# New issue orders for seven of eight attention groups, and the mixture's weights computed in the fourth group

## The reference

```python
xn = layernorm(x)
Q, K, V = heads(xn @ Wqkv); Q, K = rope(Q), rope(K)
attn = softmax(where(causal, Q @ K.T * scale, -inf))
a = (attn @ V) @ Wout + bout
probs = softmax(xn @ gate_w.T + gate_b)
weights, selected = top_k(probs, 2)
true_weights = weights * (selected < 8)
norm_w = true_weights / where(sum(true_weights) > 0, sum(true_weights), 1)
m = sum over the two selected of norm_w * (xn @ expert_w[e] + expert_b[e])
out = x + a + m
```

## Time and profile before

| what | value |
|---|---|
| median of 3 runs | 1015.39 us (1014.62 to 1016.34) |
| the profiled execution | 1015.35 us, its span 1013.6 us |
| PE, DVE, ACT, POOL busy | 90%, 83%, 72%, 46% of the span |
| groups 1 and 2 (plain, route) | 91.1 and 93.1 us |
| groups 3 to 6 (experts) | 105.8, 106.4, 106.7, 105.9 us |
| group 7 (plain) | 96.0 us |
| group 8 (last), to the last normalisation | 91.5 us |

### The profile page before, as it was taken

One profiled execution on the slowest core, in us unless ns is written; L12 is line 12 of the kernel. 1 busy time (PEld: TensorE's weight loads), 2 busy tenths in 40 slices (PEclk: granted clock), 3 DMA queues, 4 the chain that ended last, 5 costly groups with the idle time before them and its releaser, 6 DMA issues. The chain is left out here.

```text
span 1013.6 us, 22104 instructions
## 1 busy us (share of the span) xinstructions
PE 909.3 (90%) x7874; PEld 389.5 (38%) x7874; DVE 846.4 (83%) x1096; ACT 727.5 (72%) x1542; POOL 462.7 (46%) x588
## 2 busy tenths in 40 slices
PE   3888445999999999999999999999999799999988
PEld 1544311333433244344443544353434233323257
DVE  6999789899889988886888788877888599994856
ACT  3556200888778888888888788878887688799922
POOL 4677659555200343344834564255222344355610
PEclk9999765899999999999999999999999899999989
DMA  9776810300200323244413542265323321022113
GB/s 324 267 256 238 285 51 6 111 2 26 68 14 2 106 85 126 78 135 145 126 54 114 151 143 76 70 167 134 82 75 118 97 60 54 23 64 64 43 42 125
DMA packets 82084, 106.65 MB, mean 105 GB/s; under 512 B 10000, under 2 KB 59064, under 8 KB 80952
## 3 DMA queue, kind: packets, MB, share of 16 engines
q1 hardware_dynamic: 74488, 85.83, 26.3%
q0 software_dynamic: 6528, 17.83, 6.7%
q10 hardware_dynamic: 960, 1.57, 0.5%
HBM read 67.37 MB, written 37.50 MB: 103 GB/s over the span
## 5 line engine op out<-in xcount | busy, mean ns | idle before, releaser
L1272 DVE TENSOR_REDUCE blk<-psP 128x2 f32<-128x1024 f32 (+2 forms) x576 | 640.9, 1161 | 102.1 <-PE psP L1415 52.0
L1218 ACT ACTIVATE probs<-psS 128x512 f32<-128x512 f32 (+3 forms) x1280 | 589.0, 540 | 163.8 <-PE psS L1455 157.9
L1455 PE MATMUL psS<-Qs,Ks 50*128 50x512 f16 (+3 forms) x1280 | 331.6, 354 | 13.4 <-ACT probs L1218 8.9
L1415 PE MATMUL psP<-Ks,Qs 48*128 48x512 f16 (+3 forms) x1280 | 295.8, 363 | 27.9 <-DVE blk L1272 17.3
L1511 PE MATMUL psO<-probs,Vs 128*32 128x512 f32 (+3 forms) x2560 | 302.7, 548 | 11.1 <-POOL probs L1119 10.1
L1119 POOL TENSOR_SCALAR_AFFINE_SELECT probs<-probs 128x512 f32<-128x512 f32 x128 | 88.1, 689 | 333.7 <-ACT probs L1218 251.3
L1455 PEld LDWEIGHTS psS<-Qs,Ks 50*128 50x128 f16 x1280 | 96.0, 93 | 252.8 <-ACT probs L1218 157.7
L1415 PEld LDWEIGHTS psP<-Ks,Qs 48*128 48x128 f16 x1280 | 80.1, 95 | 124.1 <-DVE blk L1272 90.0
L1418 PE MATMUL psP<-later,eye 64*128 64x128 bf16 x1024 | 98.3, 223 | 0.0
L1511 PEld LDWEIGHTS psO<-probs,Vs 128*32 128x32 f32 x2560 | 52.3, 109 | 93.2 <-issue 69.3
L1418 PEld LDWEIGHTS psP<-later,eye 64*128 64x128 bf16 x1024 | 75.4, 98 | 19.9 <-issue 1.7
(11 more groups left out here) (170 smaller groups left out, 724.7 us busy)
## 6 DMA issues: line engine op xcount, KB each, us to landing
xn<-we_scratch SPq DMA_DIRECT2D x72, 256.0 KB
expert_scratch<-xn SPq DMA_DIRECT2D x36, 256.0 KB, 2.6
v_scratch<-vst SPq DMA_DIRECT2D x8, 1024.0 KB, 4.0
qk_scratch<-part SPq DMA_DIRECT2D x32, 256.0 KB, 4.0
Vs<-v_scratch SPq DMA_DIRECT2D x16, 512.0 KB, 3.9
Qs<-qk_scratch SPq DMA_DIRECT2D x168, 32.0 KB
Ks<-qk_scratch SPq DMA_DIRECT2D x168, 32.0 KB
acc<-x SPq DMA_DIRECT2D x8, 512.0 KB, 9.1
```

The costliest lines, as they stand in the source:

```text
L1218: nc.scalar.activation(probs[u % NPR][:, h, q0:CH], psS[:, k % SB, q0:CH], ACT.Exp, scale=exp_scale).then_inc(s_read[k % SB], 1)
L1272: nc.vector.tensor_reduce(out, src, AX.X, ALU.max).then_inc(item_ok[slot], 1)
L1415: ins = pe.matmul(psP[:, slot, at:at + w], Qs[r][rows, qt // CT, p, t * P:(t + 1) * P], Ks[r][rows, kc, p, 0:w], start=True, stop=True)
L1455: pe.matmul(psS[:, k % SB, q0:CH], Ks[r][rows, kt // CT, p, kt % CT * P:(kt % CT + 1) * P], Qs[r][rows, c, p, q0:CH], start=True, stop=Tru ...
```

## The change

`PE_ORDER["plain"]` (and with it route) and `PE_ORDER["experts"]` are new strings; "last" stays. They hold the same number of each letter. `weights()` is called in the fourth group (`g == 3`), behind its last item of kind `q` or `m`, and no more in the last group; `add_first()` stays where it was.

```diff
         PE_ORDER = {
             "plain": (
-                    "ss10s01ssmps10ss01ss01ss01ss10spss01s01sps0s11ss0spss10s01pss01sps0s1s0s1ssp01ss01sps10sp1s0s1s0"
...
+                    "ss10s01sspms10ss1s0s10s1ss01s0sp10sss01p01ssp01sss10ps10ssp01sss10pss0s10s1sp0ss1ps0s110sspss100"
...
             "route": "",
             "experts": (
-                    "ss1010ssmxps01s1ss0ss10s0s1spss01s1p0ssspss011sps0ssps10s10xy1s0s01xp1s0ssp0s1ss0ys10sps1x0ss1p0"
...
+                    "1s0s10ssmxps0s1s01ss1s01s0sspss01s1p0sssps10ss1ps0ssps10s10xy01sspss0101sxssp0ss101yss10ps01syx0"
...
             "last": (
...
                     else:
                         normalise(j, r, WALK.index(item[2]), item[2], slot)
+                    if g == 3 and n == rest:
+                        weights()
                     if kind == "last" and n == rest:
-                        weights()
                         add_first()
```

More of the change, by code:

```diff
@@ L924, in attend @@
             "plain": (
-                    "ss10s01ssmps10ss01ss01ss01ss10spss01s01sps0s11ss0spss10s01pss01sps0s1s0s1ssp01ss01sps10sp1s0s1s0"
-                    "sp10ssspss10s10sspms10ss10ss01ss01ps01ssp1s0ss10psss01p10sss01p0ss1s01spss1s010sspmsss1001pss10s"
-                    "s01sss01sp01sss10ps10sspsosss01ss01sp01sss10ps10ss0p1sss10psss01p01sss01psss01sss10ssps0s1s01sps"
-                    "sposs10p01sss10ps10spss10s1s0sspss01s10spmps10ss01sss01p10pssoso"),
+                    "ss10s01sspms10ss1s0s10s1ss01s0sp10sss01p01ssp01sss10ps10ssp01sss10pss0s10s1sp0ss1ps0s110sspss100"
+                    "ss1ps01ss0sss1ssmps0s10ss1s10ss0s1p0s1sp10sss01ps10s1ss0p01sss01p0s1spsss01s10sspms01ss0s1s01s1s"
+                    "0ps01ss10ssp10sss01ps10ssps01pss01s10ssp0ss1s1p0ss01spss01s10sps10ssoss10s1s0ssps01ss0ss1p0ss1sp"
+                    "1s0sposss01p10sss01p1ss0sps0s1ss10sspms0101ssspss10ss1s0pppssoos"),
             "route": "",
             "experts": (
-                    "ss1010ssmxps01s1ss0ss10s0s1spss01s1p0ssspss011sps0ssps10s10xy1s0s01xp1s0ssp0s1ss0ys10sps1x0ss1p0"
-                    "s1s01y0ss1ps01ss0sss1sspms01s0s1ss10ss01ssp01ssps1s01sp0s1s0sps1ss0pss0110xys01sps0s1s01ssxmps1s"
-                    "010sspss0s1s0s1ssps01ss10y10ss01ps10ssps0s1ssp10sss01pssos10sp01sspssx01s10sps10syss01pss01sss01"
-                    "sspss01spp1ss010yx01s10sp01sspssos10spss01psss10s01ssmyxossps10ss1s0ps1s0s1s0ppyos"),
+                    "1s0s10ssmxps0s1s01ss1s01s0sspss01s1p0sssps10ss1ps0ssps10s10xy01sspss0101sxssp0ss101yss10ps01syx0"
+                    "10ss1ps01sspss1s0ss10sssmps10s1ss0s10ss1ps0s10sps0s1sps0s10sps10s1sp01sssps10ss01xys0s1s0s1xmps0"
+                    "s1s01spss10ss10ssps0s1s01y01ss01ps10ssps10sssp01ss10spsso1ss0ps10spssx1010ssps10sy01sspss10s0s1s"
+                    "sps01sspps01s10sy01ssoxss10p1s0ss1pss010sppsss10s0s1xmyos01spsss01s1ssps0s1s0ppyos"),
             "last": (
```

## The result

| | before | after |
|---|---|---|
| median, 5 runs each on one chip | 1015.29 us (1014.62 to 1016.34) | 1019.09 us (1018.93 to 1019.87) |
| the profiled execution, its span | 1015.35, 1013.6 us | 1019.87, 1018.0 us |
| granted clock, mean | 0.959 | 0.948 |

The changed kernel is slower: the ratio of the two is 1.0032, with an interval of 1.0020 to 1.0043. The forecast of 1010.4 us was 8.7 us off and of the wrong sign; the time lies inside the range.

What follows compares the result with a forecast made beforehand. The prediction held groups without experts bound by VectorE's maxima and those with experts by TensorE's own list. Its sum was 1015.35 - 6.5 + 3.9 - 1.2 - 1.2 = 1010.4 us, range 1006.5 to 1020.5.

Steps and rivals of the forecast that it cites:

- Part 1: Last group: with the weights gone, additions end 6.4 us earlier and the mask of 959.14 is no longer held: -6.5 us.
- the first rival: Last group: the earlier additions hold a mask early, making Part 1 +3 and the time 1019.9 us; chance 0.28.
- a late one: Last group: a mask held at 953.3 or later, still a gain of 3 to 4 us, 1013.4; chance 0.12.
- Part 2: Fourth group's end: the weights delay the last normalisation, so TensorE waits for a bank of maxima: +3.9 us.
- The rival of a hidden wait: Fourth group: VectorE's 20 us idle take up the weights, +0.5 instead of +3.9, time 1007 us; chance 0.08.
- Part 3: New lists in three groups without experts: a quarter of TensorE's 1.5 us gain, -0.4 us each, -1.2 us in all.
- Part 4: New lists in four groups with experts: -0.3 us each, -1.2 us in all.
- The rival of losing lists: Seven groups lose 0.9 us each by the new lists, +6.3 instead of -2.4 us, time 1019.1 us; chance 0.10.

Runs made afterwards that it cites:

- c2: The changed kernel with one gap in the last group's additions, the 25th waiting for the 24th: 1012.50 us, one execution.
- b1: The changed kernel with the weights' 15 instructions made singly behind every fourth item of the fourth group: 1012.62 us, ratio 0.9983 to the kernel before.
- a1: The changed kernel with the weights back in the last group, so the new lists alone: 1006.31 us, ratio 0.9934 to the kernel before.
- e1: b1 with each of the last group's 32 additions waiting for the one before: 1005.41 us, ratio 0.9931 to the kernel before.
- a4: The changed kernel with the weights made twice in a row in the fourth group: 1025.66 us, one execution.
- a2: The kernel before's old lists with the weights moved to the fourth group, so the move alone: 1021.62 us, ratio 1.0090 to the kernel before.
- c1: The changed kernel with one small VectorE memset of 32 columns ahead of the last group's additions: 1021.73 us, one execution.
- d2: a1 with the last experts' rows stored ahead of the 25 loads instead of behind them: 1001.00 us, ratio 0.9863 to the kernel before.
- a3: The changed kernel with each of the last group's additions waiting for the one ahead: 1011.51 us, ratio 0.9985 to the kernel before.
- b2: b1 with the 32 additions also in pieces, one behind each item of the last group from its fifth: 1014.31 us, ratio 0.9991 to the kernel before.
- d1: a1 with each of the last group's additions waiting for the one ahead: 1010.71 us, ratio 0.9956 to the kernel before.
- d3: d2 with gaps between the last group's additions: 1003.25 us, ratio 0.9887 to the kernel before.
- d4: The kernel before with only a gap added between its 32 additions: 1018.10 us, ratio 1.0029 to the kernel before.
- e2: e1 with the last expert output of a group stored ahead of the loads that follow: 999.95 us, ratio 0.9876 to the kernel before.

## Why the prediction was wrong

**Part 1 (forecast -6.5, measured +3.9 in the last group): the step that failed is the condition "if no mask is caught earlier", and behind it the price of a held mask.** The sum assumed that the mask of 959.14 would find the additions over and that no other would be caught. One was, at 953.38, as the first rival had feared, and it fell on the late side of that rival's bound. There the prediction still promised a gain of 3 to 4 us, because TensorE would go on at 960 where it had gone on at 966. It did go on at 960.38. But in after 15.8 us of TensorE's list were still ahead at that instant (to the last transposes at 976.20), and the clock, which had fallen for 6.8 us before, stayed at half for all of them. By the table, the last group takes 81.3 us with no mask held, 84.6 with a hold of 3.77 us (c2), 88.2 with 6.95 us and 6.8 at half clock (b1), 90.5 with 6.94 and 17.1 at half (after), and 86.6 with 7.19 us near the group's end (before). So a hold costs nearly its own length, somewhat less at the very end, and up to 2.3 us more by the clock; an earlier hold is no gain, and the bound of that rival was a mistake. Its reason against, that only the mask behind a gather had been held, fell as well: in after the held one of 953.38 starts 1.0 us after the end of a gather (951.41 to 952.35), and that of a1 straight behind one passed. That the measured 1019.1 us lies in the range, and near the 1019.9 us of the first rival, is luck: that figure was for a mask held ahead of 953.3, and for a late one the prediction had 1013.4.

The size of -6.5 is near what a kernel without a held mask and with the weights gone shows: e1's last group and tail together are 125.0 us, 6.1 under before's 131.1 (e1 has gaps and pieces besides, which the changed kernel has not). But it comes from elsewhere than the prediction had it. a1, with the weights where they were, had 128.4, because its mask happened to pass: 2.7 us of gain for no edit at all in this group, and luck. The other 3.4 us are the tail, 47.1 us in a1 and 43.7 in e1: with the weights ahead of them the additions end behind TensorE's last products, a wait that the prediction does not have. What the move changed in after was the instant at which masks meet additions, and the new meeting was the dearer one.

**Part 2 (forecast +3.9, measured +5.9): the mechanism is right, the size was short by the clock.** The rows came as told: weights, then the normalisation, TensorE idle 4.12 us, the transpose late. The doubling (a4) shows that no cover exists. The missing 2 us fit the half clock of 6.8 us at 573.4, in which TensorE was busy 3.8 us at half speed, by my estimate 1.9 us lost; the prediction had priced such a drop at 1.7 us and left it in the range, out of the sum. With before's lists the same block costs 5.6 (a2). The rival of a hidden wait is refuted; and b1 shows the way in which most of it could have been hidden.

**Part 3 (forecast -1.2, measured -0.8 over groups 1, 2 and 7)** is near in sum, for partly other reasons. The lists give 0.3 in the first group, 0.3 in the second (the other 1.2 come with the old lists too, beside a half clock that did not come back), nothing in the seventh. Groups 1 and 2, forecast at 90.7 and 92.7, took 90.9 and 91.6. The seventh in after is 0.9 longer, with 10.2 us at half clock at its wait for the experts' rows instead of 6.8.

**Part 4 (forecast -1.2, measured -5.3 with the fifth group taken from a1): the term was sized from the wrong quantity.** I counted products and changes of shape, which are all but equal, and gave the 5 us of small waits a gain of 0.3 a group. The lists took 0.6 to 1.9 us off each. In the fourth group of before and of a1 TensorE made the same 986 products, its idle time fell from 2.84 to 2.23 us, and its busy time from 103.59 to 102.53. The ends of products are modelled, so the split is rough, but the larger share lies in how products overlap and follow each other, which the count had put at 0.1 us. Which part of the lists does it stays open. The rival of losing lists is refuted.

Added up: -5.0 us were forecast and +4.4 measured. Part 1 was off by +10.4, part 2 by +2.0, part 3 by +0.4, part 4 by -4.1, the start and the tail added 0.7. So the gain of part 4 hid a part of what parts 1 and 2 lost.

## What to carry to other kernels

Moving a block of work moves also all that follows it on its engine; ask what the followers will meet at their new time, and price a meeting by what it costs once it happens, not by when. A long row of two-input VectorE instructions beside GpSimd work on the critical path wants a gap in it (a wait on its own predecessor), but only where VectorE has the time for it, which is to be read from what TensorE needs of VectorE next. Small work for an engine with idle time is cheap in single pieces between its items and costs its full length, and the clock besides, as a block in front of an item that TensorE waits for.

## What the runs showed of the hardware

**A GpSimd instruction can lose to a whole row of VectorE instructions.** A mask met additions that follow each other every 0.40 us (L1366, two inputs from SBUF). Mostly it passed within 0.63 to 0.93 us and one addition took 0.85 instead of 0.47 us. In seven kernels one mask was held, until the row ended (6.94 to 7.19 us in before, after, a2, a4, b1 and c1) or until its first gap (3.77 us in c2). In a1 and d2 none was, though a mask met the same 16th addition there, and where no two additions stood back to back (a3, b2, d1, d3, d4, e1, e2) none took over 0.90 us. The Trainium skill, page "SBUF — State Buffer", section "SBUF: two separate sides", has the pair of ports go to whichever instruction starts first, for the whole instruction, while the other blocks; by that a mask would wait for one addition. The runs agree in most meetings, and not in the held ones, where the mask began in the 16th addition and sixteen more went ahead of it (eight in c2).

**Idle time is paid twice.** With 4.12 us without work came 6.8 us at half clock (1.2 GHz), with 10.19 us (a4) 13.7, with the 5.10 us of the held mask 17.1 us in after, but 6.8 in a2 and b1 at the same place with the same hold. In these 17.1 us TensorE was busy 15.0. So a stall can leave the clock low for far longer than itself; what decided between 6.8 and 17.1 is open.
